# One large kernel of attention, experts and attention: the maxima of the first attention taken bank by bank, weight chunks and gates at other places of the turn, and another order of the second attention's start

## The reference, cut to what matters

```python
x = x + attention0(layernorm(x), Wqkv, Wout)      # 16 heads of 16, rope, causal AND within 128 positions
x = x + experts(layernorm(x), ...)                # router, top 2 of 8 experts, 512 hidden, silu gate
x = x + attention1(layernorm(x), ...)             # 16 heads of 16, xpos, causal, biases
x = x + ternary(layernorm(x), weight)             # one 256 x 256 product

# attention0, for each sequence and head
allowed = (dist <= 0) & (dist >= -(w - 1))        # dist = key - query, w = 128
scores = einsum('bhqd,bhkd->bhqk', q, k) / sqrt(16)
weights = softmax(where(allowed, scores, -inf))
out = einsum('bhqk,bhkd->bhqd', weights, v)

# experts
scores = x @ Wr.T + br
idx = top_k(scores + biases_N, 2)
val = softmax(scores) at idx, divided by its sum over the two
y = sum over the two chosen of val * (silu(a) * b) @ Wl2[n],   a, b = halves of x @ Wl1[n] + bl1[n]
```

## Time and profile before

| | |
|---|---|
| median of three runs | 2978.64 us |
| the profiled execution, its time | 2977.46 us |
| its span in the profile | 2975.8 us |
| TensorE busy (matmul) | 2530.3 us, 85% |
| VectorE | 1704.9 us, 57% |
| ScalarE | 1375.7 us, 46% |
| GpSimd | 922.9 us, 31% |
| mean granted clock of TensorE | 0.927 of full speed |

### The profile page before, as it was taken

One profiled execution on the slowest core, in us unless ns is written; L12 is line 12 of the kernel. 1 busy time (PEld: TensorE's weight loads), 2 busy tenths in 40 slices (PEclk: granted clock), 3 DMA queues, 4 the chain that ended last, 5 costly groups with the idle time before them and its releaser, 6 DMA issues. The chain is left out here.

```text
span 2975.8 us, 51500 instructions
## 1 busy us (share of the span) xinstructions
PE 2530.3 (85%) x17918; PEld 1733.0 (58%) x17918; DVE 1704.9 (57%) x5704; ACT 1375.7 (46%) x2419; POOL 922.9 (31%) x863
## 2 busy tenths in 40 slices
PE   3688888888888739999999993489989999999897
PEld 2355555555565428888888882245555555555554
DVE  3566666666766334444444442576667776666751
ACT  2345555555555413333333331156555655565553
POOL 3424553345435220000000003443444443344300
PEclk7799999999999759999999996699999999999998
DMA  4555556555665367767767753454344445344420
GB/s 136 182 168 166 160 160 184 172 157 155 184 174 169 139 227 250 252 239 253 260 238 251 258 206 106 127 166 126 114 120 143 134 142 145 115 114 135 122 72 15
DMA packets 261846, 493.73 MB, mean 166 GB/s; under 512 B 25608, under 2 KB 192904, under 8 KB 251656
## 3 DMA queue, kind: packets, MB, share of 16 engines
q1 hardware_dynamic: 243736, 437.07, 47.2%
q0 software_dynamic: 17904, 54.02, 5.4%
HBM read 301.48 MB, written 188.35 MB: 165 GB/s over the span
## 5 line engine op out<-in xcount | busy, mean ns | idle before, releaser
L629 ACT ACTIVATE a_pr<-a_bank 128x512 f32<-128x512 f32 (+1 forms) x1152 | 641.6, 573 | 559.9 <-PE a_bank L999 546.0
L887 DVE CUSTOM_DVE_ANT_0 a_junk<-a_bank,a_smask 128x256 bf16<-128x256 f32 (+3 forms) x1536 | 654.7, 464 | 405.4 <-PE a_bank L1096 404.2
L1096 PE MATMUL a_bank<-a_kst,a_qst 96*128 96x256 bf16 (+3 forms) x2048 | 452.4, 295 | 81.1 <-DVE a_nmax L887 29.1
L1122 PE MATMUL a_bank<-a_qst,a_kst 98*128 98x256 bf16 (+3 forms) x2048 | 442.6, 291 | 44.5 <-ACT a_pr L629 27.1
L1140 PE MATMUL a_bank<-a_pr,a_va 128*32 128x256 f32 (+3 forms) x4096 | 358.1, 426 | 83.0 <-ACT a_pr L629 80.0
L1401 PE MATMUL e_bank<-e_xh,e_w 128*128 128x512 f32 x1248 | 391.0, 395 | 1.4 <-DVE e_xl L1382 1.4
L1096 PEld LDWEIGHTS a_bank<-a_kst,a_qst 96*128 96x128 bf16 x2048 | 171.8, 101 | 329.9 <-DVE a_nmax L887 95.2
L999 PE MATMUL a_bank<-a_mask,a_identb 128*128 128x512 bf16 (+2 forms) x1152 | 359.8, 312 | 0.0
L1122 PEld LDWEIGHTS a_bank<-a_qst,a_kst 98*128 98x128 bf16 x2048 | 182.6, 102 | 163.6 <-ACT a_pr L629 75.0
L1401 PEld LDWEIGHTS e_bank<-e_xh,e_w 128*128 128x128 f32 x1248 | 229.6, 189 | 48.7 <-DVE e_xl L1382 1.8
L1401 PE MATMUL e_bank<-e_xl,e_w 128*128 128x512 f32 x624 | 246.5, 395 | 0.0
(11 more groups left out here) (173 smaller groups left out, 4545.2 us busy)
## 6 DMA issues: line engine op xcount, KB each, us to landing
e_w<-ws_dram SPq DMA_DIRECT2D x39, 2048.0 KB, 8.8
a_parts_dram<-a_parts SPq DMA_DIRECT2D x224, 256.0 KB, 3.9
a_qst<-a_parts_dram SPq DMA_DIRECT2D x128, 384.0 KB, 7.0
a_kst<-a_parts_dram SPq DMA_DIRECT2D x128, 384.0 KB, 8.6
e_w<-ws_dram SPq DMA_DIRECT2D x39, 1024.0 KB, 6.0
a_parts_dram<-a_parts SPq DMA_DIRECT2D x32, 768.0 KB, 3.7
ws_dram<-a_ws SPq DMA_DIRECT2D x24, 1024.0 KB, 4.4
e_xg<-xs SPq DMA_DIRECT2D x39, 512.0 KB, 6.5
```

Source lines behind the costliest of these rows:

```text
L629: nc.scalar.activation(pr[b][:, h:h + per, :], TB_[at % 2][:, 0:per * w].rearrange("p (h w) -> p h w", h=per), ACT.Exp, scale=scale).then_ ...
L887: last = nc.vector.tensor_tensor_reduce(junk[:, at % 2, j * w:(j + 1) * w], SB_[at % 2][:, j * w:(j + 1) * w], smask[:, T - w:T], scale=-1 ...
L1096: last = nc.tensor.matmul(out[:, j * w:(j + 1) * w], q[0:ROWS, hh, qb * P:(qb + 1) * P], k[0:ROWS, hh, k0:k0 + w], start=not whole or j == ...
L1122: nc.tensor.matmul(out[:, j * w:(j + 1) * w], k[0:AUG, hh, b * P:(b + 1) * P], q[0:AUG, hh, q0:q0 + w], start=(j == 0), stop=False, skip_g ...
```

## The change

- In the first attention banks with several heads are now `whole` too: TensorE adds the mask over the whole bank (`mask_it` with 512 columns), and VectorE takes the maxima of the bank with one `tensor_reduce`.
- "rest" goes from GpSimd to VectorE.
- The chunks: two in each of the turns 0 to 11, none in other turns. The second of a turn is fetched at 0.62, split at 0.90 and 0.915 and stored at 0.93.
- "scatter" stands at 0.135 to 0.261 of a turn instead of 0.165 to 0.333.
- "gates" start at 0.73 instead of 0.76; the last five stand at 0.92 and later; "place" at 0.90 instead of 0.873, "exp2" at 0.757 instead of 0.789.
- In the second attention the loading, gathering, mixing and statistics of sequence 1 stand in turn -2 at -0.30 to 0.295, ahead of most of sequence 0's own steps. For all other sequences nothing changes (the two ways to choose the turn, `int(at) == back` and `(at >= 1) == back`, agree for them).

```diff
--- before.py
+++ after.py
@@ -164,18 +164,18 @@
             if routed:
                 out += [(0.28 + 0.02 * t, ("norm2", o, t)) for t in range(NT)]
                 out += [(0.18, ("y", o)), (0.54, ("turn2", o, 0)), (0.56, ("turn2", o, 1)), (0.64, ("score", o)),
-                        (0.789, ("exp2", o)), (0.873, ("place", o))]
-                out += [(0.76 + 0.0112 * k, ("gates", o, k)) for k in range(20)]
+                        (0.757, ("exp2", o)), (0.90, ("place", o))]
+                out += [(0.73 + 0.0105 * k if k < 15 else 0.92 + 0.012 * (k - 15), ("gates", o, k)) for k in range(20)]
             else:
                 out += [(0.255 + 0.015 * t, ("norm2", o, t)) for t in range(NT)]
                 out += [(0.355, ("turn2", o, 0)), (0.37, ("turn2", o, 1)), (0.41, ("last", o, 0)), (0.42, ("last", o, 1)),
                         (0.435, ("final", o, 0)), (0.445, ("final", o, 1)), (0.45, ("y", o))]
         if routed and 0 <= i - 2 < B:
-            out += [(0.165 + 0.024 * k, ("scatter", i - 2, k)) for k in range(2 * NT)]
+            out += [(0.135 + 0.018 * k, ("scatter", i - 2, k)) for k in range(2 * NT)]
         if routed:
-            for j, (at_turn, at) in enumerate(CHUNKS):
-                if at_turn == i:
-                    out += [(at, ("fetch", j)), (at + 0.14, ("high", j)), (at + 0.145, ("rest", j)), (at + 0.17, ("keep", j))]
+            for j, (fetch, high, rest, keep) in ((2 * i, (0.13, 0.27, 0.275, 0.29)), (2 * i + 1, (0.62, 0.90, 0.915, 0.93))):
+                if 0 <= j < NE * NW // WCOLS:
+                    out += [(fetch, ("fetch", j)), (high, ("high", j)), (rest, ("rest", j)), (keep, ("keep", j))]
             if i == B:
                 out.append((0.03, ("pads",)))
         if 0 <= s < B:
@@ -186,15 +186,20 @@
             if not 0 <= n < B or n == m and m and not mixed:
                 continue
             if mixed:
-                steps = [(0.48, ("load", n)), (1.07, ("aggr", n))]
+                steps = [(0.48, ("load", n)), (1.07, ("aggr", n))] if n != 1 else [(-0.30, ("load", n)), (0.295, ("aggr", n))]
                 for t in range(NT):
-                    first = 0.69 + 0.01 * t if n == 1 else 0.36 + 0.02 * t
+                    if n == 1:
+                        steps += [(0.002 + 0.005 * t, ("gather", n, 0, t)), (0.075 + 0.01 * t, ("mix", n, 0, t)),
+                                  (0.08 + 0.01 * t, ("gather", n, 1, t)), (0.23 + 0.01 * t, ("mix", n, 1, t)),
+                                  (0.275 + 0.005 * t, ("stats", n, t))]
+                        continue
+                    first = 0.36 + 0.02 * t
                     steps += [(first, ("gather", n, 0, t)), (0.775 + 0.03 * t, ("mix", n, 0, t)),
                               (0.80 + 0.03 * t if n else 0.44 + 0.02 * t, ("gather", n, 1, t)), (0.92 + 0.022 * t, ("mix", n, 1, t)),
                               (1.0 + 0.015 * t, ("stats", n, t))]
             else:
                 steps = [(0.55, ("load", n)), (0.88, ("aggr", n))] + [(0.80 + 0.02 * t, ("stats", n, t)) for t in range(NT)]
-            out += [(at - back, st) for at, st in steps if n == 0 and back or n and int(at) == back]
+            out += [(at - back, st) for at, st in steps if n == 0 and back or n and (at >= 1) == back]
         if biases and 0 <= m < B:
             out.append((0.26 if m else 0.99, ("shift", m)))
         if biases and m == 0:
@@ -470,12 +475,7 @@
                 nc.gpsimd.memset(va[i][:, :, 0:H * VW].rearrange("p t (h d) -> p t h d", h=H)[:, :, :, DH:DH + 1],
                                  1.0).then_inc(fills, 1)
             for st in order:
-                if st[0] == "rest":
-                    j = st[1]
-                    pool.wait_ge(high_done, j + 1)
-                    nc.gpsimd.tensor_tensor(ws[:, 1, :].bitcast(F32R), ws[:, 1, :], ws[:, 0, :], ALU.subtract)\
-                        .then_inc(rest_done, 1)
-                elif st[0] == "aggr":
+                if st[0] == "aggr":
                     m = st[1]
                     pool.wait_ge(var_done, m + 1)
                     pool.wait_ge(xn_done, NT * m)
@@ -694,6 +694,11 @@
                     dve.wait_ge(tern_step, 7)
                     nc.vector.tensor_scalar(tern[:, :, :], tq, 1.0, None, ALU.min).then_inc(tern_step, 1)
                     dve.wait_ge(tern_step, 8)
+                elif st[0] == "rest":
+                    j = st[1]
+                    dve.wait_ge(high_done, j + 1)
+                    nc.vector.tensor_tensor(ws[:, 1, :].bitcast(F32R), ws[:, 1, :], ws[:, 0, :], ALU.subtract)\
+                        .then_inc(rest_done, 1)
                 elif st[0] == "stats":
                     m, t = st[1:]
                     if t == 0:
@@ -877,7 +882,7 @@
                     dve.wait_ge(s_done, at + 1)
                     if g in (0, 2) and n == 0:
                         dve.wait_ge(nparts_done, max(0, 2 * s + g // 2 - 1))
-                    whole = not window and per > 1
+                    whole = per > 1
                     if whole:
                         last = nc.vector.tensor_reduce(nmax[:, qb, g * HG + h:g * HG + h + per],
                                                        SB_[at % 2][:, 0:per * w].rearrange("p (h w) -> p h w", h=per),
@@ -1090,15 +1095,16 @@
                     pe.wait_ge(max_done, max(0, at - 1))
                     out = SB_[at % 2]
                     q, k = qst[s % 2], kst[s % 2]
-                    whole = not window and per > 1
+                    whole = per > 1
                     for j in range(per):
                         hh = g * HG + h + j
                         last = nc.tensor.matmul(out[:, j * w:(j + 1) * w], q[0:ROWS, hh, qb * P:(qb + 1) * P],
                                                 k[0:ROWS, hh, k0:k0 + w], start=not whole or j == 0, stop=not whole,
                                                 skip_group_check=whole)
                     if whole:
-                        last = mask_it(out[:, 0:per * w].rearrange("p (h w) -> p h w", h=per)[:, :, w - P:],
-                                       smask[:, T - P:T].unsqueeze(1).broadcast_to([P, per, P]))
+                        set_by = w if window else P
+                        last = mask_it(out[:, 0:per * w].rearrange("p (h w) -> p h w", h=per)[:, :, w - set_by:],
+                                       smask[:, T - set_by:T].unsqueeze(1).broadcast_to([P, per, set_by]))
                     last.then_inc(s_done, 1)
                 elif st[0] == "minus" and st[3] == 1:
                     s, half = st[1:3]
@@ -1176,10 +1182,6 @@
 WCOLS = 2 * FF
 
 
-CHUNKS = [(-1, 0.25), (-1, 0.60)] + [(i, 0.13) for i in range(B - 2)] \
-    + [(i, 0.02 + 0.18 * n) for i in (B - 2, B - 1) for n in range(4)]
-
-
 def turns_of_two(fori, step, count):
 
     step(None, Seq(None, 0))
```

## The result

The changed kernel takes 2959.47 us (median of four runs, 2958.11 to 2961.78); the kernel before took 2980.48 beside it. The ratio is 0.9931, 95% interval 0.9914 to 0.9949: 21 us faster, where 44 were forecast. The profiled execution took 2959.38 us, with a span of 2957.6 against 2975.8.

What follows compares the result with a forecast made beforehand. The prediction took the loop through GpSimd and DRAM to bound the changed kernel's turns, at 59.5 us each. Its terms, -3 + 2 - 5 - 29 - 9 = -44 us, led from 2977.5 to 2934 us, range 2884 to 2966.

Steps and rivals of the forecast that it cites:

- What bounds the turn: First attention, turns 1 to 13: the loop through GpSimd and DRAM at 59.1 us, above TensorE's 55.7; 59.5 taken.
- From the stores to the maxima's landing 16.5: Last piece of the loop in a turn: from the stores to the landing of the maxima's DMA, 16.5 us.
- I add 1: Same piece of the loop: 1 us for the second chunk's fetch ahead of the stores on SP, bounds 0 and 4.4.
- 20.4, less the 3.7 that GpSimd was late, 16.6: Middle piece of the loop: from the rope's end to the stores, 16.6 us once GpSimd is in time.
- nine added masks make it 25: First piece of the loop: from the first T to the rope's end, 23 us before and 25 with masks.
- 6.2 us of TensorE a turn ... nothing less: First attention: 28 more matmuls of 512 columns add 6.2 us of TensorE a turn, with no other work hiding them.
- upper bound of a turn, 62: Turns 1 to 13: a turn takes at most 62 us, with 4.4 + 2 added, or +27 us over the turns.
- Turns 14 and 15: Last turns of the first attention, without chunks: 48.5 and 36.5 us, together -29 us (-20 to -33).
- Second start: Start of the second attention: S starts near 1883 instead of 1891.7 us, when the stack lands: -9 us (-12 to -2).
- Turn -1 and 0: Start of the first attention: -3 us (-6 to +2) without turn -1's chunks, +2 (0 to +4) in turn 0.
- TensorE sets the turn: Rival, 15%: stores and stacks land faster, so turns 1 to 13 take 55.7 us, -55 instead of -5: 2884 us.
- The doubled chunk holds up the scatters: Rival, 11%: keep and six scatters delay norm2 and an exponential, some 5 to 6 us in 11 turns: 2994 us.

Runs made afterwards that it cites:

- the masks alone: The kernel before with only the maxima changed (masks by TensorE, one reduction a bank): 2994.48 us, ratio 1.0058.
- the two fastest kernels: The kernel after with next-sequence maxima at 0.575 and 0.68, scatters as before and second chunk's store at 1.001, with and without first-attention masks: 2885.25 and 2884.09 us.
- the run with the early maxima: The kernel after with the next sequence's maxima steps at 0.575 and 0.68 of a turn instead of 0.70 and 0.78: 2930.59 us, ratio 0.9834.

## Why the prediction came out too low

*What bounds the turn: right.* First-T waits near 4 us, no PV gap, no wait of "place", TensorE alone under the loop. (TensorE alone, forecast at 55.7, was never seen: the shortest average turn of any run is 57.2.)

*"From the stores to the maxima's landing 16.5", and "I add 1": the step that failed.* It measures 19.0. The base is 17.5 by the run with the chunks as before, 1.0 more than I took; the fetch is 1.5 (bounds 0 and 4.4), 0.5 more. The fetch delays the stack by 1.7 to 1.8, and the way from the maxima's issue to the T is 0.3 shorter. I had worked 16.5 back from a mean turn, to a T that did not wait; that T really stands 15.6 behind the stores. In the kernel before, the five Ts of turns 1 to 13 that did wait for this DMA stand 17.1 to 17.9 behind the stores; the one of turn 1, with its 5.79, 17.9. Such turns were there to be read. The other eight stand at 15.6 to 16.7, so the landing came no later than that there: the distance differs from turn to turn, and the waits pick the long ones. What makes it 17.5 on average with the old chunks, when all turns wait, is in part the stack (8.1 us after the stores, 7.5 on average before) and otherwise open.

*"20.4, less the 3.7 that GpSimd was late, 16.6": 1.0 too low, by the masks.* Where GpSimd is in time and there are no added masks it does take 16.7: in turns 0 and 1 of the kernel before, and in turns 12 and 13 of the run without masks. With the masks it is 17.6 in all these turns of the kernel after, and in turns 0 and 1 of the masks alone. Four of the 28 masks stand between the ends of the two ropes, 4 x 0.22 = 0.9 us, and they make VectorE's second rope late (a wait of 1.74 us instead of 0.82). The forecast counted only the nine ahead of the first rope.

*"nine added masks make it 25": 0.7 too low on average.* The 2 us for the masks hold: 25.3 in most turns, against 23.3 before. The rest of the average is four longer turns (25.9 to 26.6), which were not taken apart.

*"6.2 us of TensorE a turn ... nothing less":* so much work, but not so much time. In the kernel before the masks cost 0.6 us a turn, and in the two fastest kernels, which differ by them, nothing.

The three pieces of the loop come to 1.5 + 1.0 + 0.7 = 3.2 a turn. I had rounded the 59.1 up by 0.4 for slow clock; that is in the measured pieces already. The upper bound of a turn, 62, does not follow from its terms: 25 + 16.6 + 16.5 + 4.4 + 2 is 64.5, and 62.3 lies within that. So a turn is 62.3 instead of 59.5, and turns 1 to 13 together (the last two, without a second chunk, with 61.4 and 58.1) are 32 us off. That is more than the whole miss.

*Turns 14 and 15: -23.7 for -29.* Turn 14 was right (48.7 for 48.5). Turn 15 took 42.2 for 36.5, at a clock of 0.92, with a PV gap of 3.92 at 1033.67, which no experiment took apart.

*Second start: -19 for -9* (15 us by the run with this part alone). The stack landed 1879.54 - 1873.98 = 5.6 us after its issue, not the median 8.6 of the earlier trace rows. That median is over all of them; the first of each series, which is the one that counts here, lands after 5.5 us by the median in the kernel before, also in the crowded turns (5.2 in turn 7). Reckoned from that attention's first product, S started 13.2 us earlier. The other 6 us came later in it and were not separated.

*Turn -1 and 0:* -5.9 + 4.4 for -3 + 2, right as a sum. The signs are right, the sizes half.

*Rivals.* "TensorE sets the turn" had against it just what turned out true. "The doubled chunk holds up the scatters" was there but hidden, as the run with the early maxima shows; with the loop open it costs 3.9 us a turn (61.7 against 57.8 with the scatters later). What the rival missed is that the doubled chunk also delays the loop itself, at a smaller price: 2.6 us a turn by the run with the old chunks.

By the Trainium skill (SBUF — State Buffer, Who interferes with whom) "rest" on VectorE could be held up by GpSimd. I took zero, and all 24 took 1.21 to 1.24 us. All but the first met GpSimd's small norm arithmetic (128x4), and the first, which met nothing, took 1.23. So they show no lock, but none of GpSimd's large additions was met in them. The mix of the earlier trace rows that did meet one took 2.65 us, where the median of its kind is 0.48.

## What to carry to other kernels

Take the length of a loop from turns in which its last wait is seen. From a turn without the wait only an upper bound can be read. Count added work in every piece of the loop, and not only ahead of its first step: four masks further on cost 0.9 us a turn. Work moved out of a crowded stretch into every turn has its price times the number of turns: 2.6 us in each here gave back what two turns had gained. And when one limit is opened, look at the next: the early maxima took 1.0% off the kernel after, with the scatters moved as well 2.4%, and then taking 6 us of TensorE's work out of each turn gave nothing.

The best versions, 2884 to 2889 us, are 3.0% to 3.1% below the kernel before and about 2.5% below the one after, and lie within each other's intervals. The simplest is the kernel after with the early maxima and the scatters as before.

## What the runs showed of the hardware

A small DMA is slow in company. The 16 KB of maxima took 7.4 us from issue to the T that waits for it, behind two pairs of stacks, four DMAs of 384 KB. The Trainium skill (DMA: Bandwidth & Descriptors, Anatomy of one DMA — SWDGE (gpsimd) path) gives a fixed part of about 2 us for that path; this transfer is issued by SP, and no run here has it alone. The store of a chunk (1 MB) lands later too: the second of a turn, issued among the stacks, takes 10.2 to 11.4 us, the first of a turn still 4.4 to 5.1. On the page, KB each and us to landing (the median over both kinds), against 4.4 of the earlier trace rows:

```profile
ws_dram<-a_ws SPq DMA_DIRECT2D x24, 1024.0 KB, 7.7
```

TensorE's clock was lower where it waited more. In 450 to 847 us it was granted at 1.00 with the early maxima and later scatters, where no wait was above 1.8 us, and at 0.96 in the same kernel without masks, which worked less and waited up to 2.3 us at a time.
